# Query projection of a perceiver block: input in four loads, weights split ahead of the norm, four banks for the norm's transposes, all group pairs written out with the side work spread over them

## The reference, cut to what matters

```python
x = x + _L0_xattn_ref(_layernorm(x), ctx_4096, mask, q_proj_w, k_proj_w, v_proj_w, o_proj_w, q_norm_w, k_norm_w)
# in _L0_xattn_ref, HEADS = 32, HEAD_DIM = 128
q = (hidden_states @ q_proj_w.T).reshape(B, Q, NUM_HEADS, HEAD_DIM).transpose(0, 2, 1, 3)
q = rmsnorm(q, q_norm_w)          # w * q / sqrt(mean(q*q) + eps)
```

## Time and profile before

| what | us |
|---|---|
| median of the runs | 2459.31 (2459.07 to 2459.84, 3 runs) |
| profiled execution | 2460.73 |
| its span | 2459.1 |
| PE busy | 2374.4 (97%) |
| DVE busy | 1959.4 (80%) |
| POOL busy | 1572.5 (64%) |
| ACT busy | 1277.3 (52%) |

### The profile page before, as it was taken

The page is one execution under the profiler, slowest core; times in us unless marked ns, Lnnn a source line. Parts: engine busy times, 40 slices in busy tenths (PEclk is TensorE's granted clock), DMA queues, the critical chain, the costliest instruction groups (busy, mean ns, idle before and its releaser), DMA issues. The chain is left out here.

```text
span 2459.1 us, 48595 instructions
## 1 busy us (share of the span) xinstructions
PE 2374.4 (97%) x18380; PEld 1729.7 (70%) x18380; DVE 1959.4 (80%) x2666; ACT 1277.3 (52%) x2066; POOL 1572.5 (64%) x1056
## 2 busy tenths in 40 slices
PE   7999999999999999999999999999999597999999
PEld 4567887788877787788877888778887344455555
DVE  6758888887888788888878878887778646898998
ACT  6845445544555445544545545554454335655664
POOL 0128887888788787788778887788778100534353
PEclk9989999999999999999999999999999798999999
DMA  6510000000001010001000000000000642221211
GB/s 216 180 51 27 25 25 25 27 26 25 25 26 31 19 33 25 17 27 30 20 27 29 28 25 26 25 27 10 10 8 10 189 151 72 95 78 60 77 43 44
DMA packets 101143, 117.69 MB, mean 48 GB/s; under 512 B 8239, under 2 KB 70831, under 8 KB 100911
## 3 DMA queue, kind: packets, MB, share of 16 engines
q1 hardware_dynamic: 98894, 107.25, 13.7%
q0 software_dynamic: 2016, 7.34, 1.1%
HBM read 96.74 MB, written 17.83 MB: 47 GB/s over the span
## 5 line engine op out<-in xcount | busy, mean ns | idle before, releaser
L178 POOL TENSOR_TENSOR p_l<-S,p_h 128x1792 f16<-128x1792 f32 x126 | 422.6, 3354 | 263.5 <-ACT p_h L452 263.5
L558 DVE SCALAR_TENSOR_TENSOR S<-pS,rk,mask 128x256 f32<-128x256 f32 x832 | 358.8, 477 | 120.5 <-PE pS L251 108.9
L251 PE MATMUL pF<-w_h,ctx_l 128*128 128x256 f16 (+1 forms) x1664 | 454.6, 273 | 0.0
L251 PE MATMUL pF<-w_h,ctx_h 128*128 128x256 f16 (+1 forms) x1664 | 454.5, 273 | 0.0
L251 PE MATMUL pF<-w_l,ctx_h 128*128 128x256 f16 (+1 forms) x1664 | 454.5, 273 | 0.0
L568 DVE TENSOR_REDUCE mx<-S 128x256 f32<-128x3328 f32 x64 | 382.9, 5983 | 2.2
L251 PE MATMUL pF<-ctx_h,w_h 128*128 128x400 f16 (+1 forms) x1024 | 341.3, 333 | 3.5 <-PEq L797 3.5
L251 PE MATMUL pF<-ctx_l,w_h 128*128 128x400 f16 (+1 forms) x1024 | 341.3, 333 | 0.0
L251 PE MATMUL pF<-ctx_h,w_l 128*128 128x400 f16 (+1 forms) x1024 | 340.5, 333 | 0.0
L434 ACT ACTIVATE v_h<-pF 128x512 f16<-128x512 f32 (+1 forms) x224 | 126.8, 566 | 385.3 <-PE pF L251 385.3
L658 POOL TENSOR_TENSOR sq_l<-sq_f,sq_h 128x400 f16<-128x400 f32 (+1 forms) x256 | 242.8, 949 | 70.7 <-ACT sq_h L426 70.7
(11 more groups left out here) (258 smaller groups left out, 5579.4 us busy)
## 6 DMA issues: line engine op xcount, KB each, us to landing
ctx_p<-ctxT_dram SPq DMA_DIRECT2D x42, 458.0 KB, 3.6
s_wst<-winG_dram SPq DMA_DIRECT2D x8, 1536.0 KB, 6.6
q_wst<-wqT_dram SPq DMA_DIRECT2D x8, 1024.0 KB, 7.9
o_scratch<-o_st SPq DMA_DIRECT2D x32, 256.0 KB, 2.4
p_ost<-o_scratch SPq DMA_DIRECT2D x16, 512.0 KB, 6.7
p_wst<-woT_dram SPq DMA_DIRECT2D x16, 512.0 KB, 7.6
s_wst<-winG_dram SPq DMA_DIRECT2D x8, 1024.0 KB, 5.2
m_wost<-woutG_dram SPq DMA_DIRECT2D x8, 1024.0 KB, 5.4
```

Of the source, the lines that this page charges most:

```text
L178: eng.tensor_tensor(p_l[:, s % 2, t0:t1, :], S[:, s % 2, t0:t1, :], p_h[:, s % 2, t0:t1, :], ALU.subtract).then_inc(pl_ok, 1)
L251: mm = pe.matmul(out, x, y, start=first and j == 0, stop=final and j == 2)
L558: ins = dve.scalar_tensor_tensor(out=S[:, s % 2, t, :].rearrange("p (r q) -> p r q", r=REP), in0=bank[:, t % 2, :].rearrange("p (r q) -> p ...
```

## The change

1. x is loaded by four DMAs of one tile each, each with its own semaphore, and DVE's bn_stats of tile t waits for load t. The wait for the norm weights stays ahead of them on DVE.
2. ACT does a Sqrt on a constant first (buffer `root`), then the high part of g0's weights, then the Sqrt of the layer norm.
3. The norm's transposes use four banks, pT and pR, so none waits for another's `tl`.
4. The hardware loops are gone: all eight groups are written out. W0 to W3 stand at t = 3 of g0 to g3, C0 to C2 at t = 3 of g4 to g6, C3 at t = 0 of g7.
5. SP issues the last context piece right after the layer norm. Then, for g2 and g3, it first waits for kv_lo and loads W2 or W3, and only then issues the weights of g2 or g3; the weights of g4 to g7 follow.

```diff
-    def vector(self, dve):
+    def vector(self, dve, x_in=None):
         for t in range(TT):
+            if x_in:
+                dve.wait_ge(x_in[t], 16)
             dve.bn_stats(self.st[:, t, :], self.x[:, t, :]).then_inc(self.moments, 1)
...
         for t in range(TT):
             pe.wait_ge(self.normed, t + 1)
-            wait(pe, self.done, t - 1)
+            wait(pe, self.done, t + 1 - len(self.banks))
...
-        ln = LayerNorm(nc, ctx, "qln", xs, ident[:, :], eps[:, 0:1], pT, (th, tl))
+        ln = LayerNorm(nc, ctx, "qln", xs, ident[:, :], eps[:, 0:1], pT + pR, (th, tl))
...
-            for j in range(2):
-                body(0, j)
-            with eng.Fori(1, GR // 2 - 1) as pair:
+            for pair in range(GR // 2):
                 for j in range(2):
                     body(pair, j)
-            for j in range(2):
-                body(GR // 2 - 1, j)
...
-            if not isinstance(pair, int):
-                return []
-            if pair == 0:
-                return [("W", j)] if t == 3 else []
-            return [[("W", 2)], [], [("W", 3)], [("C", 0)], [], [("C", 1)], [("C", 2)], [("C", 3)]][4 * j + t]
+            g = 2 * pair + j
+            return [("W" if g < 4 else "C", g % 4)] if t == (3 if g < 7 else 0) else []
...
-            sp.dma_start(xs[:, :, :], x.rearrange("(t p) c -> p t c", p=P)).then_inc(x_in, 16)
+            for t in range(TT):
+                sp.dma_start(xs[:, t, :], x[t * P:(t + 1) * P, :]).then_inc(x_in[t], 16)
...
-            with sp.Fori(1, GR // 2 - 1) as pair:
-                for j in range(2):
-                    body(pair, j)
-            for n in range(2):
-                sp.wait_ge(kv_lo, n + 1)
-                load_kv(2 + n)
             sp.wait_ge(ln.normed, TT)
             load_ctx(NCH - 1)
-            for j in range(2):
-                body(GR // 2 - 1, j)
+            for g in range(2, GR):
+                if g in (2, 3):
+                    sp.wait_ge(kv_lo, g - 1)
+                    load_kv(g)
+                body(g // 2, g % 2)
...
             act.wait_ge(consts, 2)
+            act.activation(root[:, :], eps[:, 0:1], ACT.Sqrt)
+            split(0, 0)
             ln.scalar(act)
-            split(0, 0)
```

More of the change, by code:

```diff
@@ L753, in vector_turned @@
         for t in range(TT):
-            bank = self.banks[t % 2]
+            bank = self.banks[t % len(self.banks)]
             cols = slice(t * P, (t + 1) * P)
@@ L771, in scalar_turned @@
                 act.wait_ge(self.turned, t + 1)
-                act.activation(self.out[0][:, :, t * P:(t + 1) * P], self.banks[t % 2][:, :].rearrange("p (k c) -> p k c", k=KC),
+                act.activation(self.out[0][:, :, t * P:(t + 1) * P], self.banks[t % len(self.banks)][:, :].rearrange("p (k c) -> p k c", k=KC),
                                ACT.Copy, scale=S_H).then_inc(self.high, 1)
@@ L777, in tensor @@
             pe.wait_ge(self.normed, t + 1)
-            wait(pe, self.done, t - 1)
+            wait(pe, self.done, t + 1 - len(self.banks))
             for k in range(KC):
-                mm = pe.transpose(self.banks[t % 2][:, k * P:(k + 1) * P], self.xn[:, t, k * P:(k + 1) * P], self.ident)
+                mm = pe.transpose(self.banks[t % len(self.banks)][:, k * P:(k + 1) * P], self.xn[:, t, k * P:(k + 1) * P], self.ident)
             mm.then_inc(self.turned, 1)
@@ L810, in queries @@
         nwp = sb("q_nwp", [P, 1], F32)
+        root = sb("q_root", [P, 1], F32)
         th = sb("q_th", [P, KC, ND], F16)
@@ L835, in queries @@
         pR = [ctx.enter_context(nc.psum_tensor(f"q_pR{i}", [P, 512], F32)) for i in range(2)]
-        x_in = sem("q_x_in")
+        x_in = [sem(f"q_x_in{t}") for t in range(TT)]
         nw_in = sem("q_nw_in")
@@ L1036, in _ @@
             dve.tensor_tensor(nwp[:, :], nw[:, 0:1], nw[:, 1:2], ALU.mult).then_inc(consts, 1)
-            dve.wait_ge(x_in, 16)
-            ln.vector(dve)
+            ln.vector(dve, x_in)
             def split(pair, j):
```

## The result

| | before | changed |
|---|---|---|
| median, us | 2459.31 (2457.87 to 2461.68, 7 runs) | 2467.93 (2465.34 to 2469.53, 7 runs) |
| profiled execution; its span | 2460.73; 2459.1 | 2465.34; 2463.5 |
| first product of the phase | 19.57 | 18.76 |
| first product of g2; of g3 | 44.76; 56.88 | 48.04; 66.56 |
| last product; next phase | 117.49; 127.44 | 128.84; 136.17 |

The changed kernel is slower: ratio 1.0034, 95% interval 1.0022 to 1.0045. The median moved by +8.6 us where +13.3 was forecast. The phase itself ends 8.73 later.

A forecast was written before the change was run, and what follows sets the result against it. PE, busy 97% of the span, was taken as the bound. Stalls +15.4, clock +2.2, start -1.3, wait -0.5 and end -2.5 gave +13.3 on 2459.31, so 2472.6 us; own range 2469.5 to 2476, over all cases 2465.5 to 2478.5.

The forecast's parts named there:

- Four loads, 0: At the start: loading x in four pieces gains 0, since DVE still waits first for the norm weights.
- Norm's Sqrt 0.2 later, since ACT waits for the weights ahead of it: At the start on ACT: the split ahead of the Sqrt eats the table preload's gain; reciprocal at about 11.3, 0.2 later.
- Banks and the start, 1.3 earlier: At the start: with four banks the four `tl` run in one go, first product at 18.25, gain 1.3 us.
- The 1.9 of clock: PE's first products: 1.9 us lost at half clock; denser transposes could save it, none of it was taken.
- First stall, 8.9: Before g2: its weights land at 48.15, PE begins g2 at 52.4 instead of 43.5, 8.9 us late.
- the contention: Load of g2's weights: in flight when POOL's store of g0 begins, held up 2.5 us, bounds 0 and 4.
- Second stall behind kv_lo, both together 15.4: Before g3: its weights wait for kv_lo, PE begins at 71.0 instead of 55.6; 6.5 us, both stalls 15.4.
- Clock, 2.2 behind g3 and nothing behind g2: After the stalls: PE restarts at the lower clock, costing 2.2 us in g3, nothing in g2; bounds 0 and 2.5.
- The 0.5 of waiting before g7: In the middle: PE's 0.49 us of idle time between first and last product goes, gain 0.5 us.
- End, 2.5: From last product to next phase: only the tile's own chain is left, 7.4 instead of 9.95 us, gain 2.5.
- The signs: Expected profile: first product near 18.3, g2's split at 46 to 50, idle 6 to 10 each, next phase near 140.7.
- The first rival, a clear path: In the middle: the store doesn't touch the load and the clock stays up; +8.6, or 2467.9 us; chance 0.15.

The follow-up runs named there:

- e4: e1 with x loaded in one load as in the kernel before; 2453.72 us, ratio 0.9977 to the kernel before.
- e7: e1 with the norm weights loaded ahead of x and the norm's Sqrt ahead of the weights' split on ACT; 2454.00 us, ratio 0.9974 to the kernel before.
- e6: e1 with two banks instead of four for the norm's transposes; 2457.69 us, ratio 0.9992 to the kernel before.
- e1: Changed kernel with g2's and g3's query weights issued ahead of W2, W3 and their kv_lo wait; 2454.36 us, ratio 0.998 to the kernel before.
- e9: Changed kernel with the loads of W2 and g2's weights held back on SP, issued together with POOL's store; 2475.03 us (one run).
- e3: Changed kernel with only g2's weights moved ahead of the value weights, g3's still behind kv_lo; 2461.29 us, ratio 1.0008 to the kernel before.
- e2: Kernel before with only SP's new order of loads put in; 2471.41 us, ratio 1.0049 to the kernel before.
- e8: Kernel before with all eight groups written out in place of the hardware loops; 2459.64 us, ratio 1.0001 to the kernel before.
- e5: e1 with the kernel before's side work, W2, W3 and C0 to C3 all in g6 and g7; 2458.75 us, ratio 0.9994 to the kernel before.
- e10: e7 with twelve more transposes on PE ahead of the first product; 2453.83 us, ratio 0.9979 to the kernel before.
- e11: e7 with 22 more transposes on PE ahead of the first product; 2452.41 us, ratio 0.9969 to the kernel before.

## Why the prediction came out as it did

The sign, the cause and the places were right; the size, 8.6 where 13.3 was forecast, was within the whole range and outside the forecast's own, 2469.5 to 2476. Step by step:

- *Four loads, 0*: right within some 0.3 (e4: 6.85 in the mean against 6.80, or 6.58 over all traces with one load). The Trainium skill's rule that spoke against it (SBUF - State Buffer, The DMA setup-cost knee: each transfer pays a fixed part of some 2 us) isn't borne out for loads that are in flight together: three loads more cost nothing or some 0.3 us here.
- *Norm's Sqrt 0.2 later, since ACT waits for the weights ahead of it*: right in kind. It was 0.85 later in this execution: the weights landed at 9.85 instead of 9.1 and the split is again the whole delay. The issue of four loads doesn't show as the cause: with one load and this order on ACT (e4) they landed at 9.46, with four between 9.10 and 9.85. e7 shows what the order cost.
- *Banks and the start, 1.3 earlier*: the first product was 0.8 earlier, with the banks giving 1.65 (e6) and the later reciprocal taking 0.85. The 1.9 of clock that I left in were saved in this execution (1.8). Together 2.63, measured at the turns (29.17 and 26.54). This term was mis-sized by 1.3, by a bound that I had named and not taken. It isn't a sure gain: e1, e4 and e9 have the same transposes and nearly the same pause and lost 1.7, 2.9 and 1.7 to the lower clock.
- *First stall, 8.9*: 5.9 (5.8 by PE's idle time). The term that was mis-sized is the contention: "This load is in flight when the store begins; I take 2.5". It was 0 in the changed kernel. g2's weights landed at 43.75 and not at 48.15: 2.5 for that, 1.3 for the earlier start, and 0.6 since the pair landed 7.8 behind its issue and not 8.15, and SP issued it sooner. I had taken rows of loads issued behind a store for one issued ahead of it. e9 gives that term its size where the two coincide, 3.6, and e3 some 1 us (9.1 against 8.2) where the store comes 2.8 behind the load and another load stands behind it.
- *Second stall behind kv_lo, both together 15.4*: 12.3 (66.56 against 56.88 - 2.63). The chain from one to the other held: 9.9 from the first landing to W3's issue (10.5 forecast), 8.6 from there to the landing. e2 shows the order's cost alone, e3 that the second has its own wait.
- *Clock, 2.2 behind g3 and nothing behind g2*: g3's first turn came 14.7 late where its first product was 12.3 late: 2.4.
- *The 0.5 of waiting before g7*: gone. *Loops, 0*: right (e8).
- *End, 2.5*: 2.62; e5 takes it back with 2.68.
- *The sum*: the next phase would start 13.3 late, and it was 8.7: 3.1 less of stalls and 1.3 more at the start, with 0.2 of small terms. The median moved by the same 8.6.
- *The signs*: the first product (18.76 for 18.3), the steps of g4 to g7, the lower clock behind the stalls and the end (7.33 for 7.4) came as said. The split of g2's weights at 43.75, the idle times of 5.76 and 4.82 and the next phase at 136.17 missed the 46 to 50, the 6 to 10 and the 140.7, all by the terms above.

The first rival, a clear path, gave 2467.9 for no contention and the clock up behind the stalls. The time is the same to the digit shown, but only half of its reason: the path was clear, the clock did fall, and the saved clock at the start made up for it. That the two cancel is luck.

## What to carry to other kernels

An engine that only issues transfers has a program order as well: when a load with an early need is put behind a wait that is due later, its latency comes back on the engine at the end of the chain, here 12 us in two stalls, while PE's busy time over the whole span hardly changes (2374.4 and 2371.6 us). So list for each transfer what it waits for and who needs it first. When the price of contention is read from a trace, look at which of the two was issued first and at what is queued behind it. And a preload is worth nothing if what is moved ahead with it waits for data.

## What the runs showed of the hardware that I had not expected

- While SP's loads were under way, POOL's store began late: issued at 39.20 it moved its first packets at 42.8 (changed), issued at 50.73 at 55.8 (e3) and issued at 40.45 at 45.8 (e9), so 3.6 to 5.4 us behind its issue; in the kernel before, issued at 41.84 with nothing in its way, it was 1.6 us (43.4). With the second load issued 0.1 us behind the store it took 3.6 longer (e9).
- PE's first products began at either clock. With the sixteen transposes in one go and a pause of 2.2 to 2.4 they began at the upper level in five of six traces (the changed kernel, e1, e3, e5, e9; not e4), and in two of these (e1, e9) it fell again soon (in e1 it reads 0.90 from 18 to 20 and 0.50 from 20 to 22). With the transposes in two halves they began at the lower level in all four traces (before, e2, e6, e8). The length of the pause doesn't order them: behind 3.33 they began at the upper level and fell (e7), behind twelve more transposes and 2.70 they began at the lower one (e10), and behind twenty-two more and 0.48 the clock stayed up (e11). What decides stays open.
- The landing of the first transfers scatters: the norm weights by 0.5 us with one and the same order of loads, g0's weights by 1 us (9.5 in e7, 10.5 in e10).
